# Small-tile matmuls of a window attention gathered into one stretch per turn, with the rest of the turn reordered

## Chip, cores and metric
One core of one Trainium2 chip runs the whole program in one launch. The metric is the device time of an execution in microseconds (us), lower is better; the time before is the median of three executions.

## What is computed
Two layers on x of 8 x 256 x 56 x 56 in fp32, each `x = x + layer(group_norm(x))` with 32 groups. Layer 0 is a 3x3 convolution, 256 to 256 channels, padding 1. Layer 1 is an attention within windows of 4x4 pixels (16 tokens), cut here to what matters:

```python
qkv = einsum('nchw,oc->nohw', xw, qkv_w)        # xw: the windows, n of them
pooled = avg_pool5(qkv)                         # 5x5, within the window
msq = concat([qkv, pooled], axis=1)             # 64 heads of 8 channels: q, k, v
q = relu(msq[..., :8]); k = relu(msq[..., 8:16]); v = pad(msq[..., 16:], one column of 1)
kv = einsum('ngld,nglm->ngdm', k, v)
out = einsum('ngld,ngdm->nglm', q, kv)
out = out[..., :-1] / (out[..., -1:] + 1e-15)
y = einsum('nchw,oc->nohw', out, proj_w) * inv + shift   # batch norm
```

## The kernel before, in words
The kernel writes one instruction stream per engine by hand, with semaphores between them. The images go one after the other. The convolution of an image is made of four chunks of 14 rows; each chunk takes four products (`kk` 0 to 3) on sums and differences of neighbouring columns, and each product has two halves, one for each 128 output channels (`product(v, mt)`, L306 to 324, matmuls on L319, 18 in a half). The attention of an image runs over 25 tiles of 8 windows (128 tokens), the last tile with 4 windows. The first chunk of the next image's convolution stands between the first preparations of an image's attention (`first_chunk`), the other three chunks follow the attention (`later_chunks`).

One tile asks TensorE for: keys and values (`keys_values`, L338, 6 matmuls of 512 columns into the bank BANK_KV), q (`q_of_tile`, L345, 8 matmuls into BANK_Q), pooling of the keys and values with a 0/1 matrix (`pooled`, L354, 2 matmuls, into the same BANK_KV), keys times values in two halves, plain and pooled heads (`keys_times_values`, L365, 32 matmuls of 64x32 each, banks 4 to 7), attention, q times these products (`attend`, L379, 128 matmuls of 64x32, banks 2 and 3), the transposes of the result (`turn`, L399, 4 matmuls) and the projection (`project`, L390, 16 matmuls into BANK_Q). The matmuls of L365 and L379 use the array as tiles of 64 rows and 32 columns, all others the whole array.

The work between: ScalarE copies the keys and values out (`keys_values`, L553 to 558; v is written four times, each time times the mask of a window's place, which is eight activations a tile with the pooled ones on L568, and a pair of copies of the keys on L556 and L566), raises vp_ready when the pooled ones are out, copies q (L579, L583), the transposes (`turned`, L603) and the batch norm of the projection (`batch_norm`, L595), and makes the high part of the normalized input (`split_tile`, L546). VectorE normalizes the input of a tile (`normalize_tile`, L854, `tile_low`, L862), makes the low part of the keys and values for the pooling (`kv_low_part`, L867), masks the products of keys and values (`mask`, L894), scales the pooled q (`pooled_q`, L905), and divides (`weights`, L875 and 877, `outputs`, L885). GpSimd pools q (`pool_q`) and adds the projection to the image (`add_tile`, L1073); the SyncE queue stores a row of windows when its tiles are added.

In turn s TensorE does: keys times values, first half, of tile s; q of tile s+1; transposes of tile s-1; keys and values of s+1; keys times values, second half, of s; projection of s-1; attention of s; pooling of s+1. The waits ahead of each stretch are in the function `tile(T, e, s)`. The turns of an image are three written out and 22 in a loop (`pe.Fori`); ScalarE's and VectorE's streams have all their turns written out. One buffer yb takes the batch norm's result.

Of the kernel before, what the change touches and what calls it, by code (L numbers as in the profile page):

```python
# [14 lines left out]
P = 128  # L15
# [51 lines left out]
WARM_GROUP_NORM, WARM_FIRST_TILE, WARM_START = 4, 16, 22  # L67

CONSTS = 10

# [10 lines left out]
BANK_C = ((4, 5), (6, 7))  # L81

# [21 lines left out]
LOOPED = TILES - 3  # L104
# [12 lines left out]
def build(nc, x, w_conv, w_q, w_kv, w_proj, bn, gavg, pool_m, ident, hmask, vinit, out):  # L117
    ctx = ExitStack()
    with ctx:
# [52 lines left out]
        yb = sb("yb", [P, MT, TT])  # L172
# [128 lines left out]
        def _(pe):  # L301
# [4 lines left out]
            def product(v, mt):  # L306

                kk = v % len(PRODUCTS)
                k = PRODUCTS[kk]
                if v < len(PRODUCTS):  # L310
                    pe.wait_ge(w_ready, kk + 1)
                pe.wait_ge(d_low, v + 1)
                pe.wait_ge(conv_added, 2 * v + mt + 1)
                n = 0
                for part_w, part_d in PARTS:
                    for kt in range(KT):
                        for dy in range(TAPS):
                            d0 = (kt * CONV_IN + dy) * PAIRS
                            last = nc.tensor.matmul(  # L319
                                ps[:, BANK_C[kk % 2][mt], 0:CONV_N],  # L320
                                wc[:, part_w, k, kt * TAPS + dy, mt * P:(mt + 1) * P],
                                dp[:, kk % 2, part_d, d0:d0 + CONV_N],
                                start=(n == 0), stop=(n == len(PARTS) * KT * TAPS - 1))
                            n += 1
                last.then_inc(conv_done, 1)
# [60 lines left out]
            def project(e, units):  # L386
                n = units * TT // 2
                for mt in range(MT):
                    for q in range(QUADS):
                        last = nc.tensor.matmul(ps[:, BANK_Q, mt * TT:mt * TT + n],  # L390
                                                wp[:, q, mt * P:(mt + 1) * P], at[:, q, e, 0:n],
                                                start=(q == 0), stop=(q == QUADS - 1))
                last.then_inc(proj_done, 1)
# [9 lines left out]
            def tile(T, e, s=None):  # L403

                first, final = s == 0, s == TILES - 1
                units = 1 if final else 2
                n0, n1, n2, masks = held(pe, T), held(pe, T + 1), held(pe, T + 2), held(pe, T * 2 + 2)

                pe.wait_ge(w_loaded, DMA)
                pe.wait_ge(v_ready, n1)  # L410
                keys_times_values(0, e, units)

                if not first:
                    if not final:
                        pe.wait_ge(xh_low, n2)
                        pe.wait_ge(y_ready, n0)
                        q_of_tile(1 - e)
                    pe.wait_ge(ao_ready, n0)
                    turn(2)
                if not final:  # L420
                    pe.wait_ge(vp_ready, n1)
                    keys_values(n2, 1 - e)

                pe.wait_ge(w_loaded, DMA)
                pe.wait_ge(vp_ready, n1)
                keys_times_values(1, e, units)

                if not first:
                    pe.wait_ge(at_ready, n0)
                    if not final:  # L430
                        pe.wait_ge(q_ready, n2)
                    else:
                        pe.wait_ge(y_ready, n0)
                    project(1 - e, 2)
# [7 lines left out]
                if not final:  # L442
                    pooled(n2)

            def attention(b):
                t0 = b * TILES
                pe.wait_ge(xh_low, t0 + 2)
                pe.wait_ge(q_ready, t0 + 1)
                q_of_tile(1)
                if b < B - 1:  # L450
                    pe.wait_ge(conv_added, 2 * ((b + 1) * CONV_STEPS + len(PRODUCTS)) + 4)
                tile(t0, 0, 0)
                with pe.Fori(0, LOOPED // 2) as i:
                    for e in (1, 0):
                        tile(t0 + i * 2 + (2 - e), e)
                for s in range(LOOPED + 1, TILES):
                    tile(t0 + s, s % 2, s)
# [6 lines left out]
            def first_tile(b):  # L464
                pe.wait_ge(xh_low, b * TILES + 1)
                pe.wait_ge(y_ready, b * TILES + 1)
                keys_values(b * TILES + 1, 0)
                q_of_tile(0)

            def later_chunks(b):  # L470

                for c in range(1, CONV_CHUNKS):
                    for kk in range(len(PRODUCTS)):
                        v = b * CONV_STEPS + c * len(PRODUCTS) + kk
                        product(v, 0)
                        if b >= 1 and (c, kk) == (1, 0):
                            pe.wait_ge(ao_ready, b * TILES)
                            turn(1)
# [3 lines left out]
                        if b >= 1 and (c, kk) == (1, 0):  # L482
                            last_tile(b - 1)
                        if b + 1 < B and (c, kk) == (CONV_CHUNKS - 1, 0):
                            group_sum(gn0_of(b + 1), 0)

            def first_chunk(b):
# [11 lines left out]
                product(v + 2, 1)  # L499
                product(v + 3, 0)  # L500
                product(v + 3, 1)
# [11 lines left out]
            for b in range(B):  # L513
# [3 lines left out]
                else:  # L517
# [5 lines left out]
                    keep_warm(WARM_FIRST_TILE)  # L523
                    pooled(b * TILES + 1)
                attention(b)
            pe.wait_ge(ao_ready, B * TILES)
            turn(1)
# [3 lines left out]
        def _(act):  # L531
# [57 lines left out]
            def batch_norm(b, t):  # L589
                n = tile_units(t) * TT // 2  # L590
                act.wait_ge(proj_done, b * TILES + t + 1)
                if t >= 1:
                    act.wait_ge(out_ready, b * TILES + t)
                for mt in range(MT):
                    last = nc.scalar.activation(yb[:, mt, 0:n], ps[:, BANK_Q, mt * TT:mt * TT + n],  # L595
                                                ACT.Identity, bias=bns[:, mt:mt + 1], scale=bni[:, mt:mt + 1])
# [11 lines left out]
            def attention(b):  # L608
                for s in range(TILES):
                    if s + 1 < TILES:  # L610
                        q_of_tile(b, s + 1)
                    if s >= 1:
                        turned(b, s - 1)
                    if s + 1 < TILES:
                        keys_values(b, s + 1)
# [4 lines left out]
                    if s + 1 < TILES:  # L620
                        pooled_keys_values(b, s + 1)

            def later_chunks(b):
                for c in range(1, CONV_CHUNKS):
                    for kk in range(len(PRODUCTS)):
                        v = b * CONV_STEPS + c * len(PRODUCTS) + kk
                        if b >= 1 and (c, kk) == (1, 0):
                            turned(b - 1, TILES - 1)
# [7 lines left out]
            def first_chunk(b):  # L636
# [9 lines left out]
                split(v + 4)  # L646
                split(v + 5)
# [19 lines left out]
            for b in range(B):  # L667
# [3 lines left out]
                else:  # L671
# [5 lines left out]
                    pooled_keys_values(b, 0)  # L677
                attention(b)
            turned(B - 1, TILES - 1)
# [3 lines left out]
        def _(dve):  # L683
# [84 lines left out]
            def add_product(v, mt):  # L768
# [7 lines left out]
                for e, op in {0: ((0, ALU.add),), 1: ((0, ALU.add), (1, ALU.add)),  # L776
                              2: ((0, ALU.add), (1, ALU.subtract)), 3: ((1, ALU.subtract),)}[k]:
                    last = nc.vector.tensor_tensor(pair[:, :, e], pair[:, :, e],  # L778
                                                   ps[:, BANK_C[kk % 2][mt], 0:CONV_N], op)
# [33 lines left out]
            def first_chunk(b):  # L813
# [25 lines left out]
                pooled_q(b, 0)  # L839
                add_product(v + 2, 1)  # L840

                low_parts(v + 4)
                product_inputs(v + 5)
                add_product(v + 3, 0)
                add_product(v + 3, 1)
# [65 lines left out]
            def attention(b):  # L911
                for s in range(TILES):
                    mask(b, s, 0)
                    if s + 2 < TILES:
                        normalize_tile(b, s + 2)
                    mask(b, s, 1)
                    if s + 1 < TILES:
                        kv_low_part(b, s + 1)
                    if s + 2 < TILES:
                        tile_low(b, s + 2)  # L920
                    if s + 1 < TILES:
                        pooled_q(b, s + 1)
                    weights(b, s)
                    outputs(b, s)

# [92 lines left out]
            for b in range(B):  # L1018
# [3 lines left out]
                else:  # L1022
# [9 lines left out]
                    kv_low_part(b, 0)  # L1032
                    pooled_q(b, 0)
# [3 lines left out]
        def _(pool):  # L1037
# [30 lines left out]
            def add_tile(b, t):  # L1068
                pool.wait_ge(y_ready, b * TILES + t + 2)
                for row, col, n, first in parts_of_tile(t):  # L1070
                    for mt in range(MT):
                        xrow = xs_row(b, mt, row).rearrange("p (r w c) -> p w r c", r=WS, c=WS)[:, col:col + n]
                        last = nc.gpsimd.tensor_tensor(  # L1073
                            xrow, yb[:, mt, first * TOK:(first + n) * TOK].rearrange("p (w r c) -> p w r c", r=WS, c=WS),
# [3 lines left out]
            for b in range(B):  # L1078
                pool_q(b, 0)
                for s in range(TILES):  # L1080
                    if s + 1 < TILES:
                        pool_q(b, s + 1)
# [46 lines left out]
```

## Time and profile before

| | us |
|---|---|
| median of 3 executions | 2531.64 (2530.62 to 2537.7) |
| profiled execution | 2529.08 |
| its span, first to last instruction | 2527.1 |
| TensorE busy (matmuls) | 2464.9 |
| TensorE weight loads | 2156.1 |
| VectorE busy | 1726.4 |
| ScalarE busy | 1497.3 |
| GpSimd busy | 787.7 |

The mean granted TensorE clock is 0.999 of full speed. Matmuls overlap, and their ends are modelled, so their starts are the better measure: the time of a stretch is taken from the start of its first matmul to that of the next stretch. In the rows further down, PE is TensorE's matmuls, PEld its weight loads, DVE VectorE, ACT ScalarE, POOL GpSimd.

### The profile page before, as it was taken

To read this page: it belongs to the slowest core of one execution; us is meant where nothing else is said; L and a number is where in the kernel's file an instruction comes from. 1 tells how busy PE (TensorE), PEld (TensorE's weight loads), DVE (VectorE), ACT (ScalarE), POOL (GpSimd) and SP (SyncE) were. 2 spreads that over 40 slices of the span, in tenths; PEclk is the share of its full clock that TensorE was granted. 3 is DMA by queue.
4 is the path that set the end of the run, shared out by engine and by line. 5 is a ranking of instruction groups with operands and counts; after the bars stand their busy time and mean duration, and the time that the engine had idled before them with its cause. 6 is when DMAs were issued, how large, how long until landed. Compare 5 with 4: busy or idle time off the path is not lost.

```text
span 2527.1 us, 113160 instructions
## 1 busy us (share of the span) xinstructions
PE 2464.9 (98%) x49568; PEld 2156.1 (85%) x49568; DVE 1726.4 (68%) x3609; ACT 1497.3 (59%) x3952; POOL 787.7 (31%) x2164
## 2 busy tenths in 40 slices
PE   4999999999999999999999999999999999999999
PEld 4998889888898888988889888998889978898887
DVE  8876658766587666866668666686666866665665
ACT  2148871488615885168851688427883278823887
POOL 0014430244302443034420444204441044401444
PEclk9999999999999999999999999999999999999999
DMA  4000010000100001000010000100001000000000
GB/s 163 1 2 15 19 59 12 2 18 15 65 6 5 15 18 67 1 5 19 15 67 1 9 15 17 65 1 9 19 15 63 1 13 19 15 9 2 15 19 19
DMA packets 38933, 57.74 MB, mean 23 GB/s; under 512 B 4688, under 2 KB 36304, under 8 KB 36560
## 3 DMA queue, kind: packets, MB, share of 16 engines
q1 hardware_dynamic: 38736, 55.27, 6.2%
q8 instruction: 104, 1.70, 0.3%
q14 instruction: 93, 0.76, 0.1%
HBM read 29.57 MB, written 25.69 MB: 22 GB/s over the span
## 4 chain that ended last, share of the span: by engine, by line
PE 96%; ACT 1%; DVE 1%; issue 1%; DMA 0%; POOL 0%; SPq 0%; POOLq 0%; DVEq 0%
PE ps L319 33%; PE ps L390 16%; PE ps L338 11%; PE ps L365 10%; PE ps L379 9%; PE ps L345 8%; PE ps L354 5%; PE ps L399 3%; ACT ve L568 1%; ACT ve L558 0%; PE ps L304 0%; DMA xs<-w_conv 0%; PE ps L507 0%; DVE st L717 0%; DVE kv_part L867 0%
## 5 line engine op out<-in xcount | busy, mean ns | idle before, releaser
L319 PE MATMUL ps<-dp,wc 128*128 128x392 f32 x4608 | 834.0, 341 | 2.0 <-issue 2.0
L319 PEld LDWEIGHTS ps<-dp,wc 128*128 128x128 f32 x4608 | 816.4, 188 | 3.2 <-issue 2.3
L894 DVE TENSOR_TENSOR kvm<-ps,hm 128x576 f32<-128x576 f32 (+1 forms) x400 | 296.3, 741 | 387.0 <-PE ps L365 386.8
L540 ACT CAST dp<-dt 128x896 fp32r<-128x896 f32 x128 | 120.9, 945 | 558.4 <-PE ps L319 468.0
L1044 POOL TENSOR_TENSOR qm<-qraw 128x64 f32<-128x64 f32 x200 | 61.6, 308 | 1242.8 <-ACT qraw L579 1242.8
L390 PEld LDWEIGHTS ps<-at,wp 128*128 128x128 f32 x3200 | 372.7, 191 | 43.8 <-issue 41.4
L390 PE MATMUL ps<-at,wp 128*128 128x128 f32 (+1 forms) x3200 | 409.2, 281 | 0.4 <-ACT at L603 0.4
L1073 POOL TENSOR_TENSOR xs<-yb,xs 128x128 f32<-128x128 f32 (+3 forms) x560 | 207.3, 397 | 415.4 <-ACT yb L595 415.4
L338 PE MATMUL ps<-wkv,xt 128*128 128x512 f32 x1200 | 331.7, 411 | 0.4 <-ACT ve L568 0.4
L558 ACT ACTIVATE ve<-ps,vmask 128x256 f32<-128x256 f32 x800 | 314.8, 492 | 0.0
L568 ACT ACTIVATE ve<-ps,vmaskp 128x256 f32<-128x256 f32 x800 | 313.4, 484 | 0.0
L778 DVE TENSOR_TENSOR xs<-xs,ps 128x392 f32<-128x392 f32 x384 | 201.5, 558 | 146.4 <-PE ps L319 145.2
L365 PEld LDWEIGHTS ps<-ve,kr 64*32 64x32 f32 x12544 | 170.4, 106 | 147.3 <-issue 146.4
L365 PE MATMUL ps<-ve,kr 64*32 64x144 f32 x12544 | 288.3, 289 | 4.2 <-ACT ve L568 3.2
L379 PE MATMUL ps<-kvm,qs 64*32 64x36 f32 x25088 | 256.1, 204 | 11.6 <-issue 11.6
L379 PEld LDWEIGHTS ps<-kvm,qs 64*32 64x32 f32 x25088 | 232.2, 105 | 38.0 <-issue 14.2
L867 DVE TENSOR_TENSOR kv_part<-ps,kv_part 128x512 fp32r<-128x512 f32 x200 | 138.4, 692 | 183.0 <-ACT ve L558 183.0
L338 PEld LDWEIGHTS ps<-wkv,xt 128*128 128x128 f32 x1200 | 210.4, 188 | 38.4 <-issue 1.6
L345 PEld LDWEIGHTS ps<-xh,wq 128*128 128x128 f32 x1600 | 194.7, 191 | 42.2 <-issue 41.3
L345 PE MATMUL ps<-xh,wq 128*128 128x128 f32 x1600 | 230.0, 287 | 0.0
L566 ACT ACTIVATE kr<-ps 128x256 f32<-128x256 f32 x200 | 77.3, 387 | 225.5 <-PE ps L354 225.5
L595 ACT ACTIVATE yb<-ps,bns,bni 128x128 f32<-128x128 f32 (+1 forms) x400 | 160.7, 452 | 29.8 <-PE ps L390 28.2
(87 smaller groups left out, 2882.7 us busy)
## 6 DMA issues: line engine op xcount, KB each, us to landing
out<-xs SPq DMA_DIRECT2D x224, 112.0 KB, 1.8
xs<-x SPq DMA_DIRECT2D x16, 1344.0 KB, 8.7
xs<-x SPq DMA_DIRECT2D x16, 224.0 KB, 2.7
xs<-w_conv SPq DMA_DIRECT2D x1, 2304.0 KB, 8.5
kvm<-w_kv SPq DMA_DIRECT2D x1, 512.0 KB, 14.4
wp<-w_proj SPq DMA_DIRECT2D x4, 128.0 KB, 8.0
wq<-w_q SPq DMA_DIRECT2D x1, 256.0 KB, 13.9
gav<-gavg SPq DMA_DIRECT2D x1, 64.0 KB, 8.2
```

What stands on the lines that cost most here:

```text
L319: last = nc.tensor.matmul(ps[:, BANK_C[kk % 2][mt], 0:CONV_N], wc[:, part_w, k, kt * TAPS + dy, mt * P:(mt + 1) * P], dp[:, kk % 2, part_d ...
L338: last = nc.tensor.matmul(ps[0:TT, BANK_KV, :], xt[:, part_x, e, kt, :], wkv[:, part_w, kt, :], start=(i == 0 and kt == 0), stop=(i == len ...
L345: last = nc.tensor.matmul(ps[:, BANK_Q, mt * TT:(mt + 1) * TT], wq[:, kt, mt * P:(mt + 1) * P], xh[:, e, kt, :], start=(kt == 0), stop=(kt ...
L365: last = nc.tensor.matmul(ps[32 * q:32 * q + 32, BANK_A + 2 * h + r, gg * PLACES * QW:(gg + 1) * PLACES * QW], kr[64 * r:64 * r + 64, e, k ...
L379: last = nc.tensor.matmul(ps[32 * c:32 * c + 32, BANK_O + r, (u * G + g) * QW:(u * G + g + 1) * QW], qs[64 * r:64 * r + 64, g, e, w * 32:w ...
L390: last = nc.tensor.matmul(ps[:, BANK_Q, mt * TT:mt * TT + n], wp[:, q, mt * P:(mt + 1) * P], at[:, q, e, 0:n], start=(q == 0), stop=(q == ...
L558: last = nc.scalar.activation(ve[:, t % 2, e, 0].rearrange("p (n m) -> p n m", m=DIM + 1)[:, :, 0:DIM], ps[0:TT, BANK_KV, C:2 * C].rearran ...
L568: last = nc.scalar.activation(ve[:, t % 2, e, 1].rearrange("p (n m) -> p n m", m=DIM + 1)[:, :, 0:DIM], ps[0:TT, BANK_KV, C:2 * C].rearran ...
L595: last = nc.scalar.activation(yb[:, mt, 0:n], ps[:, BANK_Q, mt * TT:mt * TT + n], ACT.Identity, bias=bns[:, mt:mt + 1], scale=bni[:, mt:mt ...
L778: last = nc.vector.tensor_tensor(pair[:, :, e], pair[:, :, e], ps[:, BANK_C[kk % 2][mt], 0:CONV_N], op)
L894: nc.vector.tensor_tensor(kvm[:, h, 0:n].rearrange("p r (g c) -> p r g c", g=2), ps[:, BANK_A + 2 * h:BANK_A + 2 * h + n, 0:2 * PLACES * Q ...
L1073: last = nc.gpsimd.tensor_tensor(xrow, yb[:, mt, first * TOK:(first + n) * TOK].rearrange("p (w r c) -> p w r c", r=WS, c=WS), xrow, ALU.add)
```

## The change

In turn s TensorE now does: attention of tile s; both halves of keys times values of tile s+1; q of s+2; transposes of s; pooling of s+2; projection of s-1; keys and values of s+3. At an image's last two turns, where there is no further q, the two halves of the product (chunk 1, kk 0) of the next image's convolution stand in q's place (not for the last image). That product writes into the banks of q and of keys and values, and the one before it (chunk 0, kk 3) into the attention's banks. The projection writes into a free part of the first two banks of keys times values, behind a wait for the mask that reads one of them. yb has two buffers. Keys, values and pooling of one tile more, and the first tile's keys times values, are made among the first chunk's products or, for the last image, behind warming matmuls (12 twice, where 16 stood). Five turns of an image are written out and 20 are in the loop. The other engines' orders follow.

```diff
-LOOPED = TILES - 3
+LOOPED = TILES - 5
+FIRST_LOOPED = 1
+def conv_bank(v, mt):
+    c, kk = v // len(PRODUCTS) % CONV_CHUNKS, v % len(PRODUCTS)
+    if (c, kk) == (0, len(PRODUCTS) - 1):
+        return BANK_O + mt
+    if (c, kk) == (1, 0):
+        return (BANK_Q, BANK_KV)[mt]
+    return BANK_C[kk % 2][mt]
...
+            def tile(T, e, s=None, v=None):
...
                 pe.wait_ge(w_loaded, DMA)
                 pe.wait_ge(masked, masks)
                 pe.wait_ge(q_ready, n1)
                 pe.wait_ge(qp_ready, n1)
-                attend(e, units)
-
-                if not final:
-                    pooled(n2)
+                if is_tile(-1):
+                    pe.wait_ge(at_ready, n0)
+                attend(e, units(0))
+
+                if is_tile(1):
+                    pe.wait_ge(w_loaded, DMA)
+                    pe.wait_ge(v_ready, n2)
+                    if is_tile(-2):
+                        pe.wait_ge(y_ready, n0)
+                    keys_times_values(0, 1 - e, units(1))
+                    pe.wait_ge(w_loaded, DMA)
+                    pe.wait_ge(vp_ready, n2)
+                    keys_times_values(1, 1 - e, units(1))
+
+                if is_tile(2):
+                    pe.wait_ge(q_ready, n2)
+                    q_of_tile(e)
+                if v is not None and not is_tile(2):
+                    if is_tile(1):
+                        pe.wait_ge(q_ready, n2)
+                        product(v, 0)
+                    else:
+                        pe.wait_ge(vp_ready, n1)
+                        product(v, 1)
+                pe.wait_ge(ao_ready, n1)
+                turn(units(0))
+                if is_tile(2):
+                    pooled(n3)
+                if is_tile(-1):
+                    if is_tile(1):
+                        pe.wait_ge(masked, own_mask)
+                    else:
+                        pe.wait_ge(y_ready, n0)
+                    project(1 - e, 2)
+                if is_tile(3):
+                    pe.wait_ge(xh_low, n4)
+                    pe.wait_ge(vp_ready, n3)
+                    keys_values(n4, 1 - e)
...
@@ later_chunks (TensorE)
+                        if b >= 1 and (c, kk) == (1, 0):
+                            continue
+                        if b >= 1 and (c, kk) == (1, 2):
+                            pe.wait_ge(y_ready, b * TILES + 1)
                         product(v, 0)
...
@@ first_chunk (TensorE)
                 product(v + 2, 1)
+                second_tile(b)
                 product(v + 3, 0)
+                pooled(b * TILES + 2)
+                pe.wait_ge(conv_added, 2 * (v + 3) + 4)
+                first_keys_times_values(b)
                 product(v + 3, 1)
...
@@ attention (ScalarE)
-                for s in range(TILES):
...
+                for s in range(-1, TILES):
+                    if s >= 0:
+                        turned(b, s)
+                    if 0 <= s < TILES - 2:
+                        pooled_keys_values(b, s + 2)
                     if s + 2 < TILES:
-                        split_tile(b, s + 2)
+                        q_of_tile(b, s + 2)
                     if s >= 1:
                         batch_norm(b, s - 1)
-                    if s + 1 < TILES:
-                        pooled_keys_values(b, s + 1)
+                    if s + 4 < TILES:
+                        split_tile(b, s + 4)
+                    if s + 3 < TILES:
+                        keys_values(b, s + 3)
...
@@ attention (VectorE)
+                normalize_tile(b, 3)
+                tile_low(b, 3)
                 for s in range(TILES):
-                    mask(b, s, 0)
...
                     weights(b, s)
                     outputs(b, s)
+                    if s + 2 < TILES:
+                        kv_low_part(b, s + 2)
+                    if s + 1 < TILES:
+                        mask(b, s + 1, 0)
+                        mask(b, s + 1, 1)
+                        pooled_q(b, s + 1)
+                    if s + 4 < TILES:
+                        normalize_tile(b, s + 4)
+                        tile_low(b, s + 4)
...
@@ GpSimd
-                for s in range(TILES):
-                    if s + 1 < TILES:
-                        pool_q(b, s + 1)
+                for s in range(-1, TILES):
+                    if s + 2 < TILES:
+                        pool_q(b, s + 2)
```

## Rows read from the trace of the kernel before

**Rows 1.** The page, chain that ended last, share of the span by engine.
```profile
PE 96%; ACT 1%; DVE 1%; issue 1%; DMA 0%; POOL 0%; SPq 0%; POOLq 0%; DVEq 0%
```

**Rows 2.** Windows, one steady turn: stretch, its us, busy us of PE, PEld, DVE, ACT, POOL.
```profile
1447.80:1455.93 8.13, 8.13 (x236) 6.59 (x239) 4.93 (x12) 6.83 (x19) 4.02 (x11) 1.00 0.08 28
```

**Rows 3.** Timeline of PE, a steady turn: start us, us, line, operation, count.
```profile
1447.09 0.73 PE L354 MATMUL ps<-kv_part,poolm 128*128 128x512 f32 x2
...
1447.75 0.72 PE L365 MATMUL ps<-ve,kr 64*32 64x144 f32 x32
1448.40 1.16 PE L345 MATMUL ps<-xh,wq 128*128 128x128 f32 x8
1449.40 0.60 PE L399 MATMUL ps<-idn,ao 128*128 128x128 f32 x4
1449.76 1.67 PE L338 MATMUL ps<-wkv,xt 128*128 128x512 f32 x6
1451.36 0.72 PE L365 MATMUL ps<-ve,kr 64*32 64x144 f32 x32
1452.01 2.05 PE L390 MATMUL ps<-at,wp 128*128 128x128 f32 x16
1453.99 1.30 PE L379 MATMUL ps<-kvm,qs 64*32 64x36 f32 x128
1455.22 0.73 PE L354 MATMUL ps<-kv_part,poolm 128*128 128x512 f32 x2
```

**Rows 4.** Waits: who waited for what, us in total, times, longest us.
```profile
PEld ps L365 <- issue: 146.4, 393, 1.3
```

**Rows 5.** Timeline of ACT, the same steady turn.
```profile
1447.86 0.39 ACT L566 ACTIVATE kr<-ps 128x256 f32<-128x256 f32 x1 [1.08 <-PE ps L354]
1448.14 1.56 ACT L568 ACTIVATE ve<-ps,vmaskp 128x256 f32<-128x256 f32 x4
1449.60 0.37 ACT L579 COPY qraw<-ps 128x256 f32<-128x256 f32 x1
...
1450.59 0.66 ACT L603 COPY at<-ps 128x256 f32<-128x256 f32 x2
...
1454.10 0.81 ACT L595 ACTIVATE yb<-ps,bns,bni 128x128 f32<-128x128 f32 x2
```

**Rows 6.** Timelines of ACT and PE, first turn of the last image.
```profile
2319.05 1.57 ACT L568 ACTIVATE ve<-ps,vmaskp 128x256 f32<-128x256 f32 x4
...
2320.67 1.66 PE L338 MATMUL ps<-wkv,xt 128*128 128x512 f32 x6 [0.39 <-ACT ve L568]
2322.26 0.72 PE L365 MATMUL ps<-ve,kr 64*32 64x144 f32 x32
```

**Rows 7.** Timelines of PE and DVE, last full turn of an image.
```profile
1600.24 1.30 PE L379 MATMUL ps<-kvm,qs 64*32 64x36 f32 x128
...
1603.17 0.66 PE L399 MATMUL ps<-idn,ao 128*128 128x128 f32 x4 [0.35 <-DVE ao L885]
...
1601.57 0.23 DVE L875 TENSOR_SCALAR den<-ps 128x64 f32<-128x64 f32 x1 [0.28 <-PE ps L379]
...
1602.42 0.69 DVE L885 TENSOR_TENSOR ao<-ps,rcp 128x512 f32<-128x512 f32 x1
1603.03 0.45 DVE L894 TENSOR_TENSOR kvm<-ps,hm 128x288 f32<-128x288 f32 x1
```

**Rows 8.** Timelines of PE and DVE, first turn of an image.
```profile
1411.43 1.29 PE L379 MATMUL ps<-kvm,qs 64*32 64x36 f32 x128 [0.96 <-issue]
1412.97 0.73 PE L354 MATMUL ps<-kv_part,poolm 128*128 128x512 f32 x2 [0.24 <-DVE kv_part L867]
...
1412.22 0.69 DVE L867 TENSOR_TENSOR kv_part<-ps,kv_part 128x512 fp32r<-128x512 f32 x1 [0.89 <-ACT ve L558]
```

**Rows 9.** Timeline of PE, where an image's turns begin and end.
```profile
1406.53 1.05 PE L345 MATMUL ps<-xh,wq 128*128 128x128 f32 x8
...
1607.53 3.48 PE L319 MATMUL ps<-dp,wc 128*128 128x392 f32 x18
```

**Rows 10.** Timeline of PE, the loop's first turn in an image.
```profile
804.53 0.26 PE L379 MATMUL ps<-kvm,qs 64*32 64x36 f32 x4 [1.06 <-issue]
```

More of the change, by code:

```diff
@@ L65 @@
 DMA = 16
-WARM_GROUP_NORM, WARM_FIRST_TILE, WARM_START = 4, 16, 22
+WARM_GROUP_NORM, WARM_FIRST_TILE, WARM_TILE, WARM_START = 4, 16, 12, 22
 CONSTS = 10
@@ L389, in project @@
                     for q in range(QUADS):
-                        last = nc.tensor.matmul(ps[:, BANK_Q, mt * TT:mt * TT + n],
+                        last = nc.tensor.matmul(ps[:, BANK_A + mt, Y0:Y0 + n],
                                                 wp[:, q, mt * P:(mt + 1) * P], at[:, q, e, 0:n],
@@ L401, in turn, with is_tile, units @@
                     last.then_inc(tr_done, 1)
[L403 to L413, printed above, removed]
-                    if not final:
[L415 to L434, printed above, removed]
+            def tile(T, e, s=None, v=None):
+                def is_tile(d):
+                    return s is None or 0 <= s + d < TILES
+                def units(d):
+                    return 2 if s is None else tile_units(s + d)
+                n0, n1, n2, n3, n4 = [held(pe, T + d) for d in range(5)]
+                masks, own_mask = held(pe, T * 2 + 2), held(pe, T * 2 + 3)
                 pe.wait_ge(w_loaded, DMA)
@@ L453, in attention @@
+                pe.wait_ge(vp_ready, t0 + 2)
+                keys_values(t0 + 3, 0)
+                if b + 1 < B:
+                    pe.wait_ge(conv_added, 2 * v + 4)
+                for s in range(FIRST_LOOPED):
+                    tile(t0 + s, s % 2, s)
                 with pe.Fori(0, LOOPED // 2) as i:
[L454 to L457, printed above, removed]
+                    for e in range(2):
+                        tile(t0 + i * 2 + (FIRST_LOOPED + e), (FIRST_LOOPED + e) % 2)
@@ L459, in last_tile @@
+                for s in range(FIRST_LOOPED + LOOPED, TILES):
+                    tile(t0 + s, s % 2, s, v)
             def last_tile(b):
@@ L646, in first_chunk @@
                 split(v + 4)
+                split_tile(b, 2)
+                keys_values(b, 1)
+                pooled_keys_values(b, 1)
                 split(v + 5)
@@ L677, in _ @@
                     pooled_keys_values(b, 0)
+                    split_tile(b, 2)
+                    keys_values(b, 1)
+                    pooled_keys_values(b, 1)
                 attention(b)
-            turned(B - 1, TILES - 1)
             batch_norm(B - 1, TILES - 1)
@@ L838, in first_chunk @@
                 add_product(v + 2, 0)
-                pooled_q(b, 0)
+                normalize_tile(b, 2)
                 add_product(v + 2, 1)
+                tile_low(b, 2)
                 low_parts(v + 4)
+                kv_low_part(b, 1)
                 product_inputs(v + 5)
                 add_product(v + 3, 0)
+                mask(b, 0, 0)
+                mask(b, 0, 1)
+                pooled_q(b, 0)
                 add_product(v + 3, 1)
@@ L1032, in _ @@
                     kv_low_part(b, 0)
+                    normalize_tile(b, 2)
+                    tile_low(b, 2)
+                    kv_low_part(b, 1)
+                    mask(b, 0, 0)
+                    mask(b, 0, 1)
                     pooled_q(b, 0)
```

68 lines of the change are left out of this document (30 added, 38 removed).

## The prediction

> **What bounds the kernel now.** I read the page's chain of waits first: TensorE makes 96% of it [rows 1]. But a busy TensorE can be one that changes its array between forms, so I then read one steady turn, as a stretch and in order of time. A turn takes 8.13 us, and TensorE has no idle time in it, while ScalarE works 6.83, VectorE 4.93 and GpSimd 4.02 us [rows 2]. Its eight stretches, from first start to first start, are: pooling 0.66, keys times values 0.65, q 1.00, transposes 0.36, keys and values 1.60, keys times values 0.65, projection 1.98, attention 1.23 [rows 3]. Three of them use the array as 64x32 tiles (L365 twice, L379), the others whole, so the array changes form six times a turn. The list of waits shows what one change costs on the weight side: 146.4 us in 393 pauses before L365, named "issue", no engine being waited for [rows 4], so 0.37 us each. The time lost on the matmul side has to come from the same stretches: with a 8.13 us turn full of matmuls there is no other place.
>
> **What the change does to a turn.** It leaves every turn's matmuls alone and puts attention and both halves of keys times values into one stretch; four of six changes of form go. Against that, pooling now stands right ahead of the projection and of the next keys and values, which share its bank (BANK_KV) and wait for vp_ready, the five ScalarE copies of pooling's result. Today keys times values, q and transposes run beside those copies; afterwards only the projection does. So I work out two numbers for a turn: TensorE by itself, and the ring through ScalarE.
>
> *TensorE alone*, terms from [rows 3]. Attention with what follows it 1.23; first half of keys times values without a change behind it 0.49 (the merged row is 0.72 long, of which the last matmul is 0.28, plus one step between groups, 0.05), second half with the change 0.65; q 1.00; transposes 0.36; pooling 0.66 less the change behind it 0.10, so 0.56; projection 1.98 less a change of 0.09 and of 0.10 for the first, 1.79; keys and values 1.50 (1.60 less the early start beside the transposes). Sum 7.58. From the other side: two round trips of about 0.36 us less than 8.13 give 7.41. I take 7.5.
>
> The row shows the price of a change: weight loads pause 0.37 us before each small stretch. The Trainium skill (TensorEngine Tiling (Array Packing), Key Properties) says that "Changing tiling mode (not just tile) drains the TensorE"; the trace agrees. By that rule alone the turn would become about 7.4 to 7.5 us, which is the first rival below.
>
> *The ring.* From the first matmul of attention of turn s to that of turn s+1: attention 1.23, keys times values 0.49 and 0.65, q 1.00, transposes 0.36 (same terms) make 3.73 to the start of pooling. From pooling's start to ScalarE's first copy it is 0.77 (1447.09 to 1447.86) [rows 3, 5]. The copies take 1.84 (1447.86 to 1448.14 + 1.56). Then TensorE is told: where keys and values waited for these same copies, it started 0.05 behind their end and needed 1.59 to the next stretch [rows 6]. Sum 3.73 + 0.77 + 1.84 + 0.05 + 1.59 = **7.98 us**. That is more than 7.5, so the ring bounds, and TensorE stands about 0.4 us a turn before keys and values. Gain per turn: 8.13 - 7.98 = 0.15.
>
> *What else could hold a turn.* Transposes need VectorE's outputs: attention starts at 1600.24, VectorE at 1601.57, it ends at 1603.11 and the transposes start at 1603.17 [rows 7], 2.93 us; TensorE arrives 3.37 after attention's start, so no wait. Pooling needs VectorE's low part of keys and values, which comes behind the outputs: 0.61 behind 2.18 is 2.79, plus 0.69, plus 0.06 to start [rows 7, 8] = 3.54 against 3.73. The projection's new wait (mask of the next tile, bank shared) is for a VectorE row of about 0.75 that starts 0.61 behind the low part: 4.15, against 4.29; nothing. Behind that wait stand keys and values, which wait longer anyway. ScalarE with VectorE makes a second ring: all its 6.83 busy us except the 0.66 of `turned`, which falls into its wait for pooling, plus low part 0.69, starts 0.04 and 0.06, pooling 0.77 = 7.73 [rows 2, 5, 8]. Below 7.98 by 0.25. Moved steps: `split_tile` now comes behind `batch_norm` on ScalarE, and VectorE's `tile_low`, which waits for it, stands ahead of the next `weights` in VectorE's queue. Counted from pooling's start, ScalarE gets there after 0.77 + 1.74 + 0.99 (q, 1449.60 to 1450.59) + 0.81 (`batch_norm`) [rows 5] and about 0.4 for the split itself, 4.7; `tile_low` adds about as much, 5.1; the next `weights` can start 7.98 - 3.73 + 1.33 = 5.6 behind pooling. It is covered by 0.5 us; were that cover gone, the outputs, then pooling would be late by the rest. `normalize_tile` needs only VectorE's slack (4.93 of 8.13). GpSimd has q ready a turn ahead, and its 4.02 us fit; the second buffer of yb only loosens it. SP's stores follow the additions one turn later, and no queue but the engines' own is moved past. ScalarE's copies of v are the same eight instructions as before (the words "spreads all of v" change nothing that I can see), cost nil.
>
> *The unknown term* is the seam between attention and keys times values, which the kernel before never has. Bounds: below, 0.02 (another group of the same form, then the ring is 7.87 us); above, what the array pays at the first tile, where attention took 1.54 instead of 1.23 to the next stretch [rows 8] although 0.24 of that is a wait for VectorE: 0.31 more, a ring of 8.29. I take what stands in 1.23 (0.13 us between the last matmul and the next), since it is the commonest row with a semaphore instruction at this place.
>
> *Image ends.* Before, from q of the second tile to the next convolution product: 1607.53 - 1406.53 = 201.0 us [rows 9]. After, the same stretch: q 1.0, keys and values 1.6, 3.8 to pooling of tile 2, 22 turns of 7.98 = 175.6 to pooling of tile 24, then rest of pooling, projection and a change 2.55; turn 23 without its convolution half: attention 1.23, the 32 small matmuls of the half tile 0.95 (estimate from 0.49 for 32), a change 0.21, transposes 0.44, projection with a change 1.98, 4.8; turn 24: attention 0.70 (half of 1.23 and the seam), two transposes 0.14, projection 1.79, 2.6; together 192.0. Ahead of it among the products: keys and values 1.4, pooling 0.66, keys times values 1.17 = 3.2. A pause of about 1.3 us inside attention of the loop's first turn (1.06 idle named issue [rows 10]; I find it in seven of eight images) I leave in. Sum 196.5, so 4.5 us an image, and 31.5 for seven. The convolution halves cost the same wherever they stand; they cover the last tile's outputs, where 0.35 us of idle time goes [rows 7].
>
> *Last image*: 24 turns x 0.15 and the warming ahead of tile 0's pooling, shorter by four matmuls (0.9), give 4.5; against it the pipeline is one tile deeper ahead (about 2.3) and at the end the projections of tiles 23 and 24 stand behind one another with a bank to be copied out between them, where today the first is over before the last transposes: about 2.2. Together nil.
>
> **Sum.** The profiled execution took 2529.1 us (span 2527.1 and 2.0 around it), the median of runs is 2531.6, 2.5 above it. 2531.6 - 31.5 = 2500.
>
> **Rivals.** *(1) TensorE alone bounds.* The ring would have to be shorter by 0.4 us, through earlier copies. For it: every term before it is a busy TensorE. Against: six of its terms are measured and none is loose by so much. A turn of 7.5 saves 0.48 x 184 turns more = 88: 2412. Chance 0.11; values half way, down to 2450, are its nearer half. *(2) Slower: the seam.* If attention's queue is short when keys times values begin, with three semaphores to be passed there, the seam costs what the first tile shows. A turn of 8.29 costs 0.31 x 184 = 57 more: 2557. It decides from 0.17 more in the seam (no gain) and 0.21 (slower by 0.3%). Against: semaphores were passed at both ends of attention for 0.13. Chance 0.12. *(3) Nothing is gained*: the copies reach vp_ready later, because `turned` ends only about 0.2 us before pooling's result, and a turn is 8.1 to 8.2: 2524 to 2539. Chance 0.11. The forecast, turns of 7.85 to 8.1, 2475 to 2524, has 0.66.
>
> A measurement of this kernel tells 0.3%, 7.6 us. Faster: 0.66 + 0.11, and a little of the edge, 0.78. Same 0.10, slower 0.12. For 8 in 10 the range goes from half way to the first rival to the edge of the third: 2445 to 2533.
>
> **What the profile of after would show.** Right: a turn of 7.9 to 8.05; L338 with an idle time of 0.3 to 0.5 us before it in each turn, released by L568; L365 right behind L379 and pauses before small stretches once a turn; ScalarE idle ahead of pooling's copies, not ahead of keys and values'. TensorE's share falls to about 94%. Wrong: no idle time before L338 and turns of 7.5 (rival 1), L379 to L365 of 1.4 us or more (rival 2), VectorE or `turned` late before pooling (rival 3), or turns that alternate.

## The result, and the profile after

The changed kernel takes 2569.7 us (median of 4, 2556.1 to 2577.5) against 2531.1 before: a ratio of 1.014, 95% interval 1.009 to 1.019. It is 1.4% slower, where 2500 and a gain were forecast, and it lies above the range. Its runs also scatter by 21 us, those of before by 7.

The page of after, with its span, busy times, instruction queues and the chain's shares; the rows in [rows 1] answer to the last line:

```profile
span 2575.4 us, 112751 instructions
...
PE 2440.0 (95%) x49576; PEld 2191.4 (85%) x49576; DVE 1695.2 (66%) x3609; ACT 1485.7 (58%) x3952; POOL 813.4 (32%) x2164
...
PEclk9999999999999999999999999999999999998998
...
q8 instruction: 133, 2.18, 0.3%
q14 instruction: 93, 0.76, 0.1%
...
PE 94%; issue 4%; ACT 1%; DVE 1%; DMA 0%; POOL 0%; SPq 0%; POOLq 0%; ACTq 0%; DVEq 0%
```

TensorE is busy for 25 us less than before, and "issue", time in which an engine waited for nothing that the profile shows, has grown from 1% to 4% of the chain. The mean granted clock fell from 0.999 to 0.984. Queue q8 brought 133 packets of instructions; before it was 104 (`q8 instruction: 104, 1.70, 0.3%` on its page).

First a steady turn, TensorE's timeline and ScalarE's, to be laid beside [rows 3, 5]:

```profile
268.39 1.30 PE L392 MATMUL ps<-kvm,qs 64*32 64x36 f32 x128
269.54 1.23 PE L378 MATMUL ps<-ve,kr 64*32 64x144 f32 x64
270.69 1.16 PE L358 MATMUL ps<-xh,wq 128*128 128x128 f32 x8
271.69 0.60 PE L412 MATMUL ps<-idn,ao 128*128 128x128 f32 x4
272.04 0.71 PE L367 MATMUL ps<-kv_part,poolm 128*128 128x512 f32 x2
272.59 2.04 PE L403 MATMUL ps<-at,wp 128*128 128x128 f32 x16
274.74 1.63 PE L351 MATMUL ps<-wkv,xt 128*128 128x512 f32 x6
276.30 1.30 PE L392 MATMUL ps<-kvm,qs 64*32 64x36 f32 x128
...
272.79 0.39 ACT L619 ACTIVATE kr<-ps 128x256 f32<-128x256 f32 x1
273.07 1.57 ACT L621 ACTIVATE ve<-ps,vmaskp 128x256 f32<-128x256 f32 x4
```

A turn is 276.30 - 268.39 = 7.91 us; 7.98 was forecast. Keys and values (L351) start 0.10 us behind the end of ScalarE's copies (273.07 + 1.57 = 274.64), 2.15 behind the projection's start, where the projection by itself needs 1.79: the ring bounds, and TensorE stands about 0.36 us. So the middle of every image is faster than before, by 0.21 us a turn (there a steady turn takes 8.12 to 8.13).

The first turns of an image are not faster. The second image, TensorE's timeline from the first attention on:

```profile
492.58 1.30 PE L392 MATMUL ps<-kvm,qs 64*32 64x36 f32 x128
493.73 0.53 PE L378 MATMUL ps<-ve,kr 64*32 64x144 f32 x17
494.84 0.98 PE L378 MATMUL ps<-ve,kr 64*32 64x144 f32 x47 [0.58 <-issue]
...
499.79 1.63 PE L351 MATMUL ps<-wkv,xt 128*128 128x512 f32 x6 [1.98 <-issue]
501.35 1.30 PE L392 MATMUL ps<-kvm,qs 64*32 64x36 f32 x128
502.49 1.19 PE L378 MATMUL ps<-ve,kr 64*32 64x144 f32 x57
505.62 0.45 PE L378 MATMUL ps<-ve,kr 64*32 64x144 f32 x7 [1.94 <-issue]
505.99 1.97 PE L358 MATMUL ps<-xh,wq 128*128 128x128 f32 x8
```

The 1.98 us before L351 are the ring, in a turn without a projection to fill it. The other two pauses (0.58 and 1.94) stand in the middle of one stretch of small matmuls, behind the 17th and the 57th of 64, where no semaphore is waited for. The second turn thus lasts 11.86 us instead of 7.91. And after the longer pause q runs at half speed: 1.97 us for what took 1.16 in the steady turn. Where an image ends it is the same, here turn 21 of the last image, which has no load of x beside it (TensorE's timeline, then the windows' row of 2538 to 2544, in which the clock, 0.72, stands behind the five engines' busy times):

```profile
2536.51 0.96 PE L378 MATMUL ps<-ve,kr 64*32 64x144 f32 x44
2539.21 0.68 PE L378 MATMUL ps<-ve,kr 64*32 64x144 f32 x20 [1.75 <-issue]
...
2538.00:2544.00 6.00, 4.79 (x40) 4.37 (x40) 2.78 (x6) 1.69 (x5) 0.64 (x2) 0.72 0.13 42
```

The DMA view shows what belongs to these places. Of the instruction queue it has 4 packets between 485 and 510 us, where the pauses are, and none at all between 525 and 635 us, in the loop's later passes:

```profile
q8 instruction: 4, 0.07, 1.2%
```

So the pauses come where code is read for the first time. The whole trace bears it out: all 29 pauses named issue ahead of small matmuls (L378 and L392), 47 us together, stand in turns 0 to 2 and 21 to 23 of an image, while turns 3 to 20, the loop's later passes, take 7.90 to 7.95 us in all eight images. One packet is 16 KB (2.18 MB in 133). A turn has 228 matmuls and as many weight loads, and run 2 below reads 289 packets more for 160 turns more, 1.8 a turn: one packet holds some 250 instructions. In the order of before the longest run of small matmuls was attention's 128 (256 instructions), now it is 192 in 2.3 us (384 instructions, one and a half packets). And five turns of an image are written out instead of three.

**Where the 48 us of the profiled executions went.** The 18 undisturbed turns of each image give 18 x 8 x 0.21 = 30 us back, so that all the rest, the first and last turns above all, lost about 78. A mean clock of 0.984 is half speed for (1 - 0.984) x 2 x 2575 = 82 us, before for 5. What half speed costs, two windows show, each almost a whole half of a convolution product:

```profile
371.40:376.90 5.50, 5.50 (x21) 5.50 (x19) 1.07 (x4) 0.00 (x0) 0.00 (x0) 0.54 0.00 0
380.00:383.25 3.25, 3.25 (x24) 3.25 (x19) 3.08 (x6) 0.21 (x1) 2.02 (x4) 1.00 0.03 10
```

Such a half takes 5.6 us at a clock of 0.54 and 3.3 at full, so two fifths of the time at half speed are lost: an estimate of some 31 us out of 77. The rest, some 47, are the pauses themselves and the ring in short turns. This split is an estimate. Of TensorE's clock this trace shows its two levels, 2.4 and 1.2 GHz (1.0 and 0.5), and that each fall but the one at the very end came in or behind a pause or a wait of 1.3 to 4.4 us. Four of them (at 185.3, 813.3, 2356.2 and 2373.2 us) followed a wait of 1.98 us before keys and values, so they belong to the deeper pipeline and not to the instructions. The Trainium skill (TensorE: Matmul & The Clock Gate, Why this matters for your kernels) warns of idle gaps between bursts that throw TensorE back to half rate; the trace agrees, with 17 stretches of 3 to 10 us at half speed where before had one of 3 and the end.

**Four turns lost a third of it.** From the attention of turn 23 to that of turn 24 it took 15.35, 13.90, 14.89 and 15.61 us in images 1, 2, 4 and 6, against 8.75 to 8.87 in the four others: some 25 us. Each of the four has a pause of 2.70 to 4.42 us while the next x is loaded, with the DMA engines busy all the time (0.99 to 1.03 in the windows of the pauses); the one of 2.70 stands inside a convolution half, behind its third matmul. In the kernel before, this load was over when turn 23 began (352.5 to 362.1, turn 23 at 364.3 in the first image); now it begins about there (362.2 to 372.0, turn 23 at 364.0). No run takes the load away. Images 3 and 5 have the load and no such pause, and run 4 below has the load at about the same place without it (364.2 to 375.3, turn 23 at 365.8 in the first image), so the load alone does not make the pause; whether it lengthens the wait for a packet stays open.

### The profile page after: what moved, and what is told of

It is laid out like the page before. It is cut to its first block, busy times and chain, and to the rows that moved or that the text cites. A ratio compares the mean times of both kernels' runs of the same rounds, so it can differ in the third digit from the quotient of the medians.

```text
span 2575.4 us, 112751 instructions
## 1 busy us (share of the span) xinstructions
PE 2440.0 (95%) x49576; PEld 2191.4 (85%) x49576; DVE 1695.2 (66%) x3609; ACT 1485.7 (58%) x3952; POOL 813.4 (32%) x2164
## 3 DMA queue, kind: packets, MB, share of 16 engines
q8 instruction: 133, 2.18, 0.3%
## 4 chain that ended last, share of the span: by engine, by line
PE 94%; issue 4%; ACT 1%; DVE 1%; DMA 0%; POOL 0%; SPq 0%; POOLq 0%; ACTq 0%; DVEq 0%
PE ps L332 32%; PE ps L403 14%; PE ps L351 13%; PE ps L392 9%; PE ps L378 9%; PE ps L358 8%; PE ps L367 4%; PE ps L412 3%; PE ps L317 1%; ACT ve L621 0%; DMA xs<-w_conv 0%; PE ps L559 0%; DVE st L773 0%; PE ps L343 0%; ACT yb L648 0%
## 5 line engine op out<-in xcount | busy, mean ns | idle before, releaser
L332 PE MATMUL ps<-dp,wc 128*128 128x392 f32 x4608 | 847.7, 343 | 4.9 <-issue 4.8
L351 PE MATMUL ps<-wkv,xt 128*128 128x512 f32 x1200 | 329.6, 410 | 36.7 <-issue 20.8
L923 DVE TENSOR_TENSOR xt<-xh,xt 128x256 fp32r<-128x256 f32 x200 | 86.2, 431 | 411.0 <-ACT xt L599 410.9
L656 ACT COPY at<-ps 128x256 f32<-128x256 f32 (+1 forms) x400 | 129.0, 372 | 348.9 <-PE ps L412 348.6
L611 ACT ACTIVATE ve<-ps,vmask 128x256 f32<-128x256 f32 x800 | 328.4, 558 | 0.0
L392 PEld LDWEIGHTS ps<-kvm,qs 64*32 64x32 f32 x25088 | 233.1, 106 | 85.0 <-issue 82.3
L351 PEld LDWEIGHTS ps<-wkv,xt 128*128 128x128 f32 x1200 | 212.9, 190 | 104.4 <-issue 67.9
L378 PE MATMUL ps<-ve,kr 64*32 64x144 f32 x12544 | 256.0, 287 | 38.7 <-issue 34.5
L955 DVE TENSOR_TENSOR kvm<-ps,hm 128x576 f32<-128x576 f32 (+1 forms) x400 | 279.5, 738 | 17.6 <-PE ps L378 17.3
L392 PE MATMUL ps<-kvm,qs 64*32 64x36 f32 x25088 | 258.0, 205 | 13.1 <-issue 12.6
L1140 POOL TENSOR_TENSOR xs<-yb,xs 128x128 f32<-128x128 f32 (+3 forms) x560 | 200.6, 385 | 129.1 <-ACT yb L648 129.1
L378 PEld LDWEIGHTS ps<-ve,kr 64*32 64x32 f32 x12544 | 195.7, 106 | 48.0 <-issue 47.7
L648 ACT ACTIVATE yb<-ps,bns,bni 128x128 f32<-128x128 f32 (+1 forms) x400 | 171.1, 509 | 50.7 <-PE ps L403 50.7
```

Source lines behind the costliest of these rows:

```text
L332: last = nc.tensor.matmul(ps[:, conv_bank(v, mt), 0:CONV_N], wc[:, part_w, k, kt * TAPS + dy, mt * P:(mt + 1) * P], dp[:, kk % 2, part_d, ...
L351: last = nc.tensor.matmul(ps[0:TT, BANK_KV, :], xt[:, part_x, e, kt, :], wkv[:, part_w, kt, :], start=(i == 0 and kt == 0), stop=(i == len ...
L378: last = nc.tensor.matmul(ps[32 * q:32 * q + 32, BANK_A + 2 * h + r, gg * PLACES * QW:(gg + 1) * PLACES * QW], kr[64 * r:64 * r + 64, e, k ...
L392: last = nc.tensor.matmul(ps[32 * c:32 * c + 32, BANK_O + r, (u * G + g) * QW:(u * G + g + 1) * QW], qs[64 * r:64 * r + 64, g, e, w * 32:w ...
L611: last = nc.scalar.activation(ve[:, t % 2, e, 0].rearrange("p (n m) -> p n m", m=DIM + 1)[:, :, 0:DIM], ps[0:TT, BANK_KV, C:2 * C].rearran ...
L648: last = nc.scalar.activation(yb[:, t % 2, mt, 0:n], ps[:, BANK_A + mt, Y0:Y0 + n], ACT.Identity, bias=bns[:, mt:mt + 1], scale=bni[:, mt: ...
```

## The experiments

**1. The old order, with more turns written out.** Only the number of looped turns changes; every engine does the same work in the same order.

```diff
-LOOPED = TILES - 3
+LOOPED = TILES - 5
```

> The kernel before with 5 turns of an image written out instead of 3 (20 looped instead of 22), nothing else. Theory (instructions): TensorE pauses where it reads turns' code for the first time, because the small matmuls ask for instructions faster than they are brought (16 KB packets, 256 instructions, one per 3.5 us or more in the changed kernel's trace). Two more first-read turns per image in the old order, whose longest run of small matmuls is 128, not 192: some pauses of 1 to 2 us per image, 8 to 30 us in all, about 29 more packets of the instruction queue, 2540 to 2562 us. Rival (order and data waits at the ends made the loss): 2531 within 3.

Measured: 2562.1 us (2557.3 to 2563.1), at the upper edge of what was expected, ratio 1.012 (1.010 to 1.014), 133 packets instead of 104. The packets are on its page; TensorE's timeline has a pause inside attention at an image's end:

```profile
q8 instruction: 133, 2.18, 0.3%
...
671.53 0.29 PE L379 MATMUL ps<-kvm,qs 64*32 64x36 f32 x13 [2.60 <-issue]
```

The number of written-out turns alone, at two more an image, costs 31 us, as much as four fifths of what the whole change lost. The clock fell to 0.992 with it. The rival, that the new order's waits at the image ends made the loss, can't explain this run, whose order is the old one. The pause shown, and the run's two others of about 3 us (ending at 986.0 and 1615.0), stand while x is loaded or 1 us behind it, and one of 2.42 at 1116.8 has no load beside it.

**2. No loop at all, in both orders.** The loop is taken out and its turns are written out.

> The kernel before without the loop, all 25 turns written out. Theory: with 1.84 packets of 256 instructions asked for per turn of 8.13 us and one per 3.5 to 4 us brought, the mean fits but bursts do not always: 0.3 to 1.3 us in each of 160 more first-read turns, 2580 to 2740 us. Rival (no supply bound): 2531 within 5.

> The changed kernel without the loop. Theory (instructions): every turn behaves as its turns 1, 2 and 21 do now, 8.9 to 9.6 us instead of 7.91, so 160 x 1.0 to 1.7 more, 2730 to 2840 us, clock at half speed in many places. Rival (ends and data waits): turns of 7.91 as before, 2570 within 10.

Measured, one execution each: 2623.3 us in the old order and 2756.1 in the new one. The chain's shares and the instruction queue of the new one, the queue's line in the old one, and two turns of the new one's timeline:

```profile
q8 instruction: 392, 6.42, 1.0%
...
PE 89%; issue 9%; ACT 1%; DVE 1%; DMA 0%; POOL 0%; SPq 0%; POOLq 0%; ACTq 0%; DVEq 0%
...
1200.76 1.30 PE L392 MATMUL ps<-kvm,qs 64*32 64x36 f32 x128
1201.90 0.98 PE L378 MATMUL ps<-ve,kr 64*32 64x144 f32 x48
1204.81 0.48 PE L378 MATMUL ps<-ve,kr 64*32 64x144 f32 x16 [1.92 <-issue]
...
1212.00 1.30 PE L392 MATMUL ps<-kvm,qs 64*32 64x36 f32 x128
```

```profile
q8 instruction: 393, 6.44, 1.0%
```

Both are the same amount of code, 392 and 393 packets. The old order loses 92 us in 160 turns that are read for the first time in place of out of the loop, 0.6 each; the new order 186 us in 144, 1.3 each, and its turn above takes 11.2 instead of 7.91. The code of a turn is the same, and its turns are 3% shorter, so the new order loses twice as much by the same instructions. That points at the long run of small matmuls; run 3 tests it. The Trainium skill (Runtime: NRT & Kernel Launch, Instruction fetch mechanics) has blocks of 16 KiB that the sequencer fetches ahead while it executes, and says that the cost is "mostly hidden" and that "kernels prefer full unrolling where possible". The blocks agree with the packets here; that unrolling is to be preferred does not: here it costs 4% and 7%, and the measurement decides.

**3. The long run split where code is new.** In the written-out turns keys times values (`next_products`) stand behind q (or the convolution half); the looped turns stay as they are.

```diff
...
+                if s is None:
+                    next_products()
                 if is_tile(2):
                     pe.wait_ge(q_ready, n2)
                     q_of_tile(e)
...
+                if s is not None:
+                    next_products()
                 pe.wait_ge(ao_ready, n1)
```

> The changed kernel, but in its five written-out turns keys times values stand behind q (or behind the product's half), so that the runs of small matmuls are 128 and 64 long there as in the old order; the looped turns are left alone. Theory (instructions): the pauses inside and behind attention in turns 21 to 24 and 0 shrink from about 5 us an image to 1 or 2, and with them some of the half clock: 2530 to 2555 us; turns 1 and 2 stay slow. Rival (data waits): two changes of form more in five turns, 2572 to 2580.

Measured: 2543.5 us (2533.2 to 2552.5), ratio to before 1.0046 (1.002 to 1.007). Two more changes of form in each of 40 turns, and still 26 us faster than the changed kernel, with the same 133 packets: the run's length is worth that much in five turns an image.

**4. Fewer turns written out in the new order.** From the second image on turns 0 to 21 are looped and three are written out. Turn 0 then has a projection to make, of stale data; it fills time in which TensorE waited for the ring anyway.

```diff
-                for s in range(FIRST_LOOPED):
+                first, looped = (0, LOOPED + 2) if b else (FIRST_LOOPED, LOOPED)
+                for s in range(first):
...
-                act.wait_ge(proj_done, b * TILES + t + 1)
+                act.wait_ge(proj_done, b * TILES + t + 1 + b)
```

> The changed kernel with 22 turns of an image in the loop (0 to 21) and 3 written out, from the second image on; turn 0 makes one projection more there, of stale data that nobody reads, while it waits for ScalarE's copies anyway. Theory (instructions): two first-read turns less in each of seven images, at about 2 us each as the runs with 5 instead of 3 written out have it: about 30 us less, 2535 to 2548, and 26 packets less of the instruction queue. Rival (order at the image ends): 2570 within 6.

Measured: 2520.9 us (2516.4 to 2524.8), ratio 0.997 (0.996 to 0.998), and 108 packets. That is 49 us less than the changed kernel and more than the 30 forecast: 3.5 for each of 14 first-read turns, with the clock back at 0.998 in the profiled execution. Not all of it need be the instructions. The run changes a second thing: turn 0's wait of 1.98 us, behind which the clock fell at 813.3 and 2373.2 in the changed kernel, is filled by the added projection. Its trace has 14 us at half speed, where the changed kernel's has 82. It beats the kernel before by 0.3%.

**5. Both remedies.**

> Both remedies: 22 turns looped, and in the written-out turns keys times values behind q. If the pauses for instructions are the loss, the two add up as far as they do not meet in the same turns: 2510 to 2528 us, under the kernel before (2531). Rival: no more than the better of the two alone, 2540.

Measured: 2516.3 us (2507.3 to 2531.8), ratio 0.995 (0.994 to 0.997). They add up a little only; the two intervals overlap, and whether the split still helps here is not settled by them.

**6. The convolution halves back out of the end turns.**

> The changed kernel with the convolution halves back behind the attention instead of in turns 23 and 24. Theory (instructions): a product's half asks for 36 instructions in 3.3 us and lets the supply catch up, so without it the small matmuls of turns 21 to 24 stand closer: 2570 to 2600 us. Rival (the halves in the end turns are themselves the loss, by waits on their banks): 2540 to 2560.

Measured: 2583.2 us (2576.7 to 2587.4), ratio 1.020 (1.019 to 1.022), some 14 us slower than the changed kernel. The halves in turns 23 and 24 are a gain, not the loss. Whether by the few instructions that they need (36 in 3.3 us) or by covering the last tiles' outputs, this run doesn't separate.

**7. The ring cut.** Two of the four masked copies of the pooled v are left out, so that half of the pooled values are not those of the reference.

```diff
-                for e in range(PLACES):
+                for e in range(PLACES // 2):
```

> The changed kernel with two of the four masked copies of the pooled v left out (so half of the windows' pooled values are stale or zero): 0.71 us less between pooling and the next keys and values. Ring theory: the steady turn falls from 7.91 to TensorE's own 7.4 to 7.55, and the idle time before L351 goes. Rival (something else sets 7.91, the array itself or VectorE): 7.8 to 7.9.

Measured: 2491.0 us, one execution. Its steady turn on TensorE:

```profile
1212.53 1.30 PE L392 MATMUL ps<-kvm,qs 64*32 64x36 f32 x128
1213.68 1.23 PE L378 MATMUL ps<-ve,kr 64*32 64x144 f32 x64
...
1216.73 2.04 PE L403 MATMUL ps<-at,wp 128*128 128x128 f32 x16
1218.53 1.64 PE L351 MATMUL ps<-wkv,xt 128*128 128x512 f32 x6
1220.10 1.30 PE L392 MATMUL ps<-kvm,qs 64*32 64x36 f32 x128
```

The turn is 7.57 us. The chain of the ring was right, and TensorE alone is 7.57, where the terms summed to 7.58 and I took 7.5.

**8. A whole kernel with the short ring.** ScalarE copies the pooled v out once, which frees the bank, and the four masked copies are made from that copy, two on ScalarE and two on VectorE. The kernel is otherwise that of run 4, and in a second run that of run 5.

```diff
+                nc.scalar.copy(vraw[:], ps[0:TT, BANK_KV, C:2 * C]).then_inc(v_out, 1)
...
+            def pooled_values(b, t):
+                dve.wait_ge(v_out, b * TILES + t + 1)
+                for e in range(PLACES // 2, PLACES):
+                    last = nc.vector.tensor_scalar(...)
...
-                    pe.wait_ge(vp_ready, n3)
+                    pe.wait_ge(v_out, n3)
```

> The run with 22 looped turns, and the ring shortened without leaving work out: ScalarE copies the pooled v out once, unmasked, and gives the bank free behind that (1.1 us earlier); two masked copies are then made from there by ScalarE and two by VectorE. Ring theory: the ring falls to about 6.8 us, TensorE alone bounds, the steady turn is 7.57 as in the run with two copies left out; 0.34 us in some 180 turns is 60 us, so 2521 - 60 = 2461, range 2450 to 2480, with the pauses for instructions as they are or a little longer. Rival (VectorE, 0.7 us busier, or ScalarE becomes the bound): turns of 7.7 to 8.0, 2490 to 2530.

> The same with keys times values behind q in the written-out turns: 5 us less than the run without that, as between the two runs with 22 looped turns: 2445 to 2475. Rival (instruction supply now bounds, since 470 instructions a turn come closer together): no difference between the two.

Measured: 2471.4 us (2459.4 to 2471.6), ratio 0.974 (0.972 to 0.976), and with the split 2460.5 (2451.5 to 2464.6), ratio 0.972 (0.970 to 0.973); the two intervals overlap, so the split's gain is again not settled. The latter's timelines, a turn of TensorE and the copies on ScalarE:

```profile
1215.87 1.30 PE L395 MATMUL ps<-kvm,qs 64*32 64x36 f32 x128
...
1220.07 2.04 PE L406 MATMUL ps<-at,wp 128*128 128x128 f32 x16
1221.86 1.65 PE L354 MATMUL ps<-wkv,xt 128*128 128x512 f32 x6
1223.44 1.30 PE L395 MATMUL ps<-kvm,qs 64*32 64x36 f32 x128
...
1220.55 0.37 ACT L633 COPY vraw<-ps 128x256 f32<-128x256 f32 x1
1220.94 0.91 ACT L636 ACTIVATE ve<-vraw,vmaskp 128x256 f32<-128x256 f32 x2
```

Again 7.57 us; keys and values (L354) now stand 1.79 behind the projection, without a wait, and VectorE, busier by about 126 us in all, is not in the way. With all its work this kernel beats the one before by 2.8% and the changed one by 4.2%.

## Why the prediction was wrong

**The steady turn was right.** 7.98 forecast, 7.91 measured; runs 7 and 8 show the ring and, without it, TensorE's own 7.57. The seam between attention and keys times values, the term called unknown, is 1.15 - 1.10 = 0.05 us (L392 to L378 1.15, of which attention's own matmuls are 1.10 by the 1.23 of [rows 3] less the 0.13 of the forecast), near its lower bound, 0.02: rival 2's mechanism did not come. With 0.05 in place of the 0.13 that was taken, the ring's sum is 7.90. The other estimate of TensorE alone, two round trips of 0.36 less, 7.41, was too low: a round trip gave back (8.13 - 7.57) / 2 = 0.28. VectorE's outputs and `tile_low` hold nothing up; the projection's weight loads wait for the mask in 155 turns, 0.3 us at most, ahead of the longer wait for the ring.

**The step that failed** stands in *Image ends*: "A pause of about 1.3 us inside attention of the loop's first turn (1.06 idle named issue [rows 10]; I find it in seven of eight images) I leave in." It was seen, it stood in the middle of a run of small matmuls with no engine waited for, and it was carried over as a constant, though the change touches both things that it hangs on: more turns read for the first time (two more an image; 31 us in run 1, in the old order) and a run of small matmuls half as long again where they stand (26 us back when it is split there, run 3; twice the loss per turn in run 2). The 192.0 us of an image's stretch was a sum of durations without a term for bringing instructions. With the pause of 1.3 it was 193.3; measured from q of the second tile to the product behind the projection of tile 23, less 6.6 for the two convolution halves in between, it is 201.8, the mean of seven images (197.5 to 205.1). These 8.5 us an image make 60 of the some 80 us by which the profiled execution missed the forecast. In run 4 the same stretch takes 194.9. (The pause itself was read a little large: the loop's first turn in the kernel before is 0.4 to 1.6 us longer than a steady one in seven images, 1.1 on the mean.) Looking at where the pause stood beside the instruction queue's packets would have shown it.

**The second omission** is the clock. The text of the prediction has no term for it, since before it was 0.999. The pauses pull it down, for an estimated 31 us here. That they also make the runs scatter is likely and not tested.

**The last image**, which was to cost nothing more, took 14.7 us more. From the first group sum ahead of its attention to the end it is 221.7 us before (from 2305.4) and 236.4 after (from 2339.0); 8.0 of the 14.7 lie ahead of its first attention, where 6.8 and 3.4 us run at half speed against 3.4 before. In run 4 the same stretch is 223.8.

**The price of a first-read turn** isn't one number: 1.9 us in run 1, 0.6 and 1.3 in run 2, 3.5 in run 4 (turn 0's filled wait included). The pauses stand at different matmuls in each image, and what follows them at half speed differs. I don't settle what fixes their places, nor what the loads of x that run beside some of them add, the longest ones in turn 23 above all; the last two images have no loads and have the pauses too.

**The rivals**: slower came true with another mechanism than the one priced; "TensorE alone" is real, at 7.57, once the ring is cut.

## What to carry to other kernels

Code outside a loop has a price of its own when it is made of many short instructions, here 0.6 to 3.5 us a turn of 456: count the instructions of each stretch beside the time it takes, and look for "issue" pauses inside stretches, with the instruction queue's packets beside them. When a steady turn is made shorter by a deeper pipeline, the turns that fall out of the loop at both ends can cost more than the loop gains, so loop them too, even with a dummy stretch. And a ring through another engine can be cut where a bank is freed: copy out once, and do the rest from the copy.

## What the runs showed that was not expected

That one copy of 0.37 us in place of four frees the bank early enough to take the ring out altogether: 50 us between runs 4 and 8. Some 180 turns of 0.34 less would be 61; the profiled execution of run 8 has 38 us at half speed against 14 in run 4, which may be the rest. That a stale projection in turn 0 is free: where no pause falls into it, turn 0 takes 8.19 to 8.22 us with it and without it. And that TensorE's half speed comes with pauses of only some 2 us here: a pause of 1.94 us was followed by q at 1.97 us instead of 1.16. The 1.98 of the ring just before it, at 499.79, was not followed by slower matmuls (L351 took 1.63), while the same 1.98 in the first image was (L351 at 184.67 took 2.36).
